# Joining the last stage of a two-layer graph kernel to its product stage, and starting that stage's gathers inside the layers

## The reference, cut to what matters

```python
def graph_conv(x, W, b):                      # three of these in a row, relu after the first two
    m = (x @ W)[src] * norm_src[:, None]
    return segment_sum(m, dst) * norm_dst[:, None] + b
x = layernorm(x + graph_conv3(x))             # (v - mean) / sqrt(var + 1e-5)

bf  = exp(coeff * (dist[:, None] - centers) ** 2)
bf  = ssp(bf @ V1 + c1); bf = ssp(bf @ V2 + c2)      # ssp(z) = softplus(z) - ln 2
msg = x[src] * edge_attr * bf * cutoff(dist)
agg = segment_prod(msg, dst)                  # product over a node's edges
x = layernorm(x + ssp(agg @ V3 + c3))
```

## Time and profile before

| | us |
|---|---|
| median of 3 runs | 4655.83 (4644.31 to 4661.99) |
| the profiled execution | 4661.2 |
| its span, first to last instruction | 4659.4 |

### The profile page before, as it was taken

How to read it: one execution, slowest core, us unless ns; L and a number is a source line. 1 busy time by engine, 2 the same in 40 slices (tenths; PEclk the granted TensorE clock), 3 DMA queues, 4 the chain that set the end, 5 groups by cost and what they waited for, 6 DMA issues and landing times. The chain is left out here.

```text
span 4659.4 us, 67064 instructions
## 1 busy us (share of the span) xinstructions
PE 3628.6 (78%) x23091; PEld 2344.5 (50%) x23091; DVE 3161.9 (68%) x5677; ACT 2724.9 (58%) x4265; POOL 1914.3 (41%) x1883
## 2 busy tenths in 40 slices
PE   5888889899999999999998566666666666666663
PEld 4777777444554455444544344444444444444442
DVE  9999999423333233332312788888888888888886
ACT  3666665322222222222200899999999989999983
POOL 6222000401000000100011677777777777777774
PEclk9888888999999999999999778788777778878775
DMA  4333333778887888887875666666666666666762
GB/s 139 131 134 131 124 129 129 239 242 250 247 248 225 245 246 245 249 247 243 248 229 167 193 198 194 199 195 202 197 195 200 199 195 199 195 198 194 201 186 76
DMA packets 641678, 920.75 MB, mean 198 GB/s; under 512 B 69714, under 2 KB 423239, under 8 KB 641431
## 3 DMA queue, kind: packets, MB, share of 16 engines
q1 hardware_dynamic: 550727, 782.85, 52.2%
q0 software_dynamic: 59936, 119.71, 10.9%
q10 hardware_dynamic: 30768, 15.26, 1.2%
HBM read 674.96 MB, written 242.59 MB: 197 GB/s over the span
## 5 line engine op out<-in xcount | busy, mean ns | idle before, releaser
L1311 POOL DMA_INDIRECT hgat<-x_rows,edge_src x1564 | 1504.6, 962 | 490.1 <-issue 475.1
L953 PE MATMUL bank<-gran,hp 128*128 128x490 bf16 x7056 | 1504.1, 372 | 28.6 <-DVE hp L1098 28.6
L953 PEld LDWEIGHTS bank<-gran,hp 128*128 128x128 bf16 x7056 | 677.3, 96 | 822.7 <-DVE hp L1098 30.1
L815 POOL DMA_INDIRECT x_sb<-h_rows,last_i x147 | 138.7, 943 | 1503.6 <-DMA h_rows<-h_out 1469.1
L1388 PE MATMUL bank<-c_b,one_b 96*128 96x512 bf16 x309 | 140.2, 454 | 744.4 <-DVE efl L1454 677.1
L1439 DVE TENSOR_SCALAR bank<-rows_e,edge_same,edge_first 128x128 f32<-128x128 f32 x1564 | 645.1, 412 | 42.5
L611 PEld LDWEIGHTS bank<-hi_hot,lo_hot 128*128 128x128 bf16 x7840 | 546.0, 155 | 217.8 <-issue 69.6
L611 PE MATMUL bank<-hi_hot,lo_hot 128*128 128x49 bf16 x7840 | 574.1, 219 | 94.7 <-DVE hi_hot L403 93.4
L527 ACT CAST stage<-bank 128x490 bf16<-128x490 f32 x784 | 451.9, 577 | 308.1 <-PE bank L611 297.4
L1019 DVE TENSOR_SCALAR t<-bank,c_sb 128x512 f32<-128x512 f32 x82 | 61.6, 751 | 826.3 <-PE bank L928 816.6
L1388 PEld LDWEIGHTS bank<-c_b,one_b 96*128 96x128 bf16 x309 | 30.5, 99 | 1019.9 <-issue 984.1
(11 more groups left out here) (237 smaller groups left out, 4485.9 us busy)
## 6 DMA issues: line engine op xcount, KB each, us to landing
gran<-step_counts SPq DMA_DIRECT2D x336, 857.5 KB, 4.9
dist<-weight_by_step SPq DMA_DIRECT2D x391, 256.0 KB, 4.6
running_products<-rows_e SPq DMA_DIRECT2D x391, 256.0 KB, 3.7
step_counts<-stage SPq DMA_DIRECT2D x112, 857.5 KB
ef<-in_edge_attr SPq DMA_DIRECT2D x391, 224.0 KB, 4.2
hgat<-x_rows,edge_src POOLq DMA_INDIRECT x1564
kn<-keep_and_norm_of_steps SPq DMA_DIRECT2D x48, 490.0 KB, 6.8
edge_filter_times_attr<-g_out SPq DMA_DIRECT2D x82, 256.0 KB, 3.5
```

The lines of the kernel that those rows point to most:

```text
L953: last = nc.tensor.matmul(y, hp[:, 7 * g + i, part, :], gran[:, g, :, i * IS:(i + 1) * IS], start=first, stop=last_)
L1311: pool.indirect_dma_start(out=hgat[:, b % U, c, :], out_offset=None, in_=x1_d, in_offset=bass.IndirectOffsetOnAxis(ap=edge_src[:, b, c:c + ...
```

## The change

- `hp1` loses its third part to a tile of its own, `third`, which outlives the layer stage; `hgat`, the ring of gathered rows, now lies in that tile's memory. Which part is meant is asked of `split_of`.
- At the end of the layer stage POOL waits until all of `x1_rows` is stored and then issues the 24 gathers of the ring's first six blocks (`gather_block`), still in the layer stage's `Block`. The product stage's POOL program starts at block 6.
- The late tiles 35 to 48 are cut at tile 45 (`LATE`, the first tile that needs the last block). `layer_norm` of tiles 35 to 41 and 42 to 44 moves into the last block, their root follows, and their ten tiles are normalised right after the last block's rows are biased; only four tiles stay behind the last gathers. There are eight stores of `x1_rows`.
- Roots: `exp(-0.5 * ln(var + eps))` on ACT, two instructions from the table that is loaded anyway; the add and the reciprocal on DVE and the square root go, in both stages. In the last stage there is one root per group.
- The last stage loses its own `Block` and stands behind the product stage's work in the same one; its loads of `v3` and `c3` come ahead of SP's last waits. `soft` now shares the memory of `prod`.
- In the last stage DVE normalises group g - 2 between `biased(g)` and `residual(g - 1)`.

```diff
+        U = 6
+        third = sb("third_of_hp1", [P, NT, D], BF16)
+        hgat = third[:].rearrange("p t d -> p (t d)").bitcast(F32)[:, 0:U * C4 * D].rearrange(
+            "p (u c d) -> p u c d", u=U, c=C4)
+        def gather_block(pool, b):
+            for c in range(C4):
+                pool.indirect_dma_start(out=hgat[:, b % U, c, :], out_offset=None, in_=x1_d,
+                                        in_offset=bass.IndirectOffsetOnAxis(ap=edge_src[:, b, c:c + 1], axis=0)
+                                        ).then_inc(s_gt[b % U], 16)
...
-            CUTS = (0, 35, NT)
+            LATE = next(t for t in range(NT) if blocks_for(t) == BLOCKS)
+            NORMS = [(7 * q, 7 * q + 7) for q in range(NG7 - 1)] + [(7 * NG7 - 7, LATE), (LATE, NT)]
+            ROOTS = ((0, 5), (5, 7), (7, 8))
...
+                    pool.wait_ge(s_x1d, 16 * len(NORMS))
+                    for b in range(U):
+                        gather_block(pool, b)
...
                     def root(i):
-                        act.wait_ge(s_rv, i + 1)
-                        nc.scalar.activation(rstd[:, CUTS[i]:CUTS[i + 1]], rstd[:, CUTS[i]:CUTS[i + 1]], ACT.Sqrt
-                                             ).then_inc(s_sd, 1)
+                        a, b = cuts(i)
+                        act.wait_ge(s_bn, 2 * ROOTS[i][1])
+                        nc.scalar.activation(rstd[:, a:b], mom[:, a:b, 1], ACT.Ln, bias=eps[:]).then_inc(s_lv, 1)
+                        act.wait_ge(s_lv, i + 1)
+                        nc.scalar.activation(rstd[:, a:b], rstd[:, a:b], ACT.Exp, scale=-0.5).then_inc(s_sd, 1)
...
+                            if n == 3 * BLOCKS - 1 and g == NG7 - 1:
+                                layer_norm(5)
+                                layer_norm(6)
                     post(At(3 * BLOCKS - 1))
                     bias_rows(2, At(3 * BLOCKS - 1))
-                    layer_norm(5)
-                    layer_norm(6)
-                    reciprocals(1)
                     normalise(1)
+                    layer_norm(7)
+                    normalise(2)
...
-                    for b in range(NB):
-                        if b >= U:
-                            pool.wait_ge(s_v, b - U + 1)
+                    for b in range(U, NB):
+                        pool.wait_ge(s_v, b - U + 1)
...
+                        gather_block(pool, b)
...
+                    for g, (a, b) in enumerate(groups):
+                        for t in range(a, b):
+                            pool.indirect_dma_start(out=prod[:, t, :], out_offset=None, in_=run_d,
...
+                    copy_turned(0)
+                    for g in range(NG):
+                        if g + 1 < NG:
+                            copy_turned(g + 1)
+                        softplus(g)
+                        if g:
+                            root(g - 1)
+                    root(NG - 1)
...
-        with ExitStack() as ph:
-            with nc.Block() as block:
...
                     for g in range(NG):
                         biased(g)
+                        if g >= 2:
+                            normalise(g - 2)
                         if g:
                             residual(g - 1)
-                        for i in range(2):
-                            if g == BATCHES[i][1]:
-                                reciprocals(i)
-                            if BATCHES[i][1] < g <= BATCHES[i][1] + 4:
-                                normalise(i, g - BATCHES[i][1] - 1 + BATCHES[i][0])
+                    normalise(NG - 2)
                     residual(NG - 1)
-                    reciprocals(2)
-                    for g in range(*BATCHES[2]):
-                        normalise(2, g)
+                    normalise(NG - 1)
```

More of the change, by code:

```diff
@@ L670, in gnn @@
             s_hst = [sem(f"s_h_stored{r}") for r in range(2)]
-            s_xg = [sem(f"s_x_gathered{q}") for q in range(NG7)]
+            s_xg = [sem(f"s_x_gathered{q}") for q in range(NG7 + 1)]
             s_hm, s_p1, s_h1, s_p2, s_hp = (sem(n) for n in (
@@ L694, in gnn, with split_of @@
             assert all(blocks_for(7 * q + 6) <= b - 1 for b, q in PARTS_AT.items())
+            def split_of(k, tiles, part):
+                if k % 2 == 0:
+                    return hp0[:, tiles, part, :]
+                return hp1[:, tiles, part, :] if part < 2 else third[:, tiles, :]
             class At:
@@ L911, in _ @@
                                     store_x1(q)
+                                root(1)
                     copy_h(2, At(BLOCKS * 3 - 1))
                     store_h(At(BLOCKS * 3 - 1), At(BLOCKS - 1))
-                    root(1)
-                    for q in range(5, NG7):
+                    for q in range(5, 7):
                         store_x1(q)
-                    act.wait_ge(s_x1d, 16 * NG7)
+                    root(2)
+                    store_x1(7)
+                    act.wait_ge(s_x1d, 16 * len(NORMS))
                     for r in range(2):
@@ L1096, in rest_h @@
                         dve.wait_ge(ready, NG7 * k + q + 1)
-                        into = part if nth == 0 else hps[k % 2][:, 7 * q:7 * q + 7, 2, :]
-                        nc.vector.tensor_tensor(into, part, hps[k % 2][:, 7 * q:7 * q + 7, nth, :], ALU.subtract
+                        into = part if nth == 0 else split_of(k, slice(7 * q, 7 * q + 7), 2)
+                        nc.vector.tensor_tensor(into, part, split_of(k, slice(7 * q, 7 * q + 7), nth), ALU.subtract
                                                 ).then_inc(signal, 1)
@@ L1241, in gnn @@
             s_fi = [sem(f"s_efl_in{r}") for r in range(U)]
-            s_gt = [sem(f"s_hgat{r}") for r in range(U)]
             s_rst = [sem(f"s_run_stored{r}") for r in range(U)]
@@ L1404, in _ @@
                     nc.tensor.transpose(banks[7][:, 0:P], ct[:, 0:P], ident[:]).then_inc(s_ctt, 1)
+                    pe.wait_ge(s_v3, 16)
+                    pe.wait_ge(s_x14, ND)
+                    pe.wait_ge(s_r1, ND)
+                    pe.wait_ge(s_r2, ND)
+                    pe.wait_ge(s_fin, ND)
+                    for g, (a, b) in enumerate(groups):
+                        pe.wait_ge(s_pg[g], 16 * (b - a))
+                        if g >= 2:
+                            pe.wait_ge(s_ptc, g - 1)
+                        for t in range(a, b):
+                            last = nc.tensor.transpose(banks[g % 2][:, (t - a) * P:(t - a + 1) * P], prod[:, t, :],
+                                                       ident[:])
+                        last.then_inc(s_pt, 1)
+                        pe.wait_ge(s_ptc, g + 1)
+                        if g >= ZB:
+                            pe.wait_ge(s_zs, g - ZB + 1)
+                        for t in range(a, b):
+                            last = nc.tensor.matmul(banks[2 + g % ZB][:, (t - a) * D:(t - a + 1) * D],
+                                                    prodT[:, g % 2, (t - a) * P:(t - a + 1) * P], v3_sb[:],
+                                                    start=True, stop=True)
+                        last.then_inc(s_z, 1)
                 @block.vector
```

217 lines of the change are left out of this document (79 added, 138 removed).

## The result

The changed kernel takes 4662.38 us in the median (4656.27 to 4668.47), the kernel before beside it 4655.51: ratio 1.0015, 95% interval 1.0008 to 1.0021. The forecast was 1.3 us faster; it became 6.9 us slower. The profiled execution of the changed kernel took 4663.31 us, with a span of 4661.5, against 4661.2 and 4659.4 before.

A forecast was written before the change was run, and what follows sets the result against it. The prediction took POOL's gather issue to pace the product stage and the last stage until its last gather. Its terms +3.6 - 3.2 - 1.7 = -1.3 us took the median 4655.8 to 4654.5 us, range 4642 to 4670.

The forecast's parts named there:

- part 2: Seam from layers to product stage: early gathers delay the barrier, POOL's 25th gather 3.6 us later, bounds 0.2 to 11.5.
- part 3: Seam to the last stage: next gather waits only for the scatter's landing, 3.2 us sooner, bounds 0 to 3.5.
- Part 1: End of the layer stage: only four tiles behind the last gathers, last store 4.1 us sooner.
- No second pause: Product stage: after its one hole POOL does not wait again; ACT and DVE catch up within 60 to 90 blocks.
- Part 4: Behind the last gather: fewer tiles left to normalise, 1.7 us less, bounds 0 to 3.5; removed table loads worth nothing.
- Rival (d): End of the kernel: output's way out bounds the tail, so nothing is gained there, 4656 us; chance 0.05.
- Rival (a): Product stage: the 29 us start lag of ACT and DVE stays, +24 us, 4680 us; chance 0.07.
- Rival (b): First seam: barrier is cheap and early gathers pay, some 5 us ahead, -9.6 us, 4646 us; chance 0.10.
- Rival (c): POOL's gathers change length as DVE's work beside them shifts phase, 28 us less, 4627 us; chance 0.06.

The follow-up runs named there:

- e12: Changed kernel with the loads of `v3` and `c3` moved to the start of the product stage; 4656.87 us, ratio 1.0003 to the kernel before.
- the control: The changed kernel run once more, unaltered, on the chip of other runs; 4666.41 us, ratio 1.0011 to the kernel before.
- e5: Changed kernel without early gathers and without POOL's wait for the `x1_rows` stores; 4652.43 us, ratio 0.9983 to the kernel before.
- e2: Changed kernel without early gathers, POOL's wait for the last `x1_rows` stores kept, on a slow chip; ratio 1.0002 to the kernel before.
- e10: Changed kernel without early gathers, POOL's wait for the last `x1_rows` stores kept, again on a slow chip; ratio 1.0000 to the kernel before.
- e13: Changed kernel without early gathers, POOL's store wait kept, on a chip where POOL sets the pace; ratio 0.9992 to the kernel before.
- e4: Changed kernel with POOL also waiting for its 24 early gathers to land before the barrier; 5045.61 us, one execution on a slow chip.

## Why the prediction was wrong

**The step that failed is the restart in part 2.** "I take 2.9 from the nearest row; ends: 0.4 (2598.0) and, if it counts from the last gather's landing, 4.2 (2601.8)": the barrier took 8.0 us, beyond both ends. From the last residual add, the 25th gather was forecast at +46.3 us and came at +52.4. The early gathers ended 1.3 us sooner than forecast (36.0 for 37.3 us behind the add), the barrier took 5.1 us more, and from the stage's start to the 25th gather it took 8.4 us for 6.1, since the first block's filter, issued behind four other loads, landed at 2609.1. The row I went by was the seam to the last stage, where POOL's DRAIN takes 2.5 us; in the layers' `Block` it already took 5.8 us behind the last gather in the kernel before, unseen because nobody waited, and 7.75 with 24 gathers more. The price of being last is not one number for every `Block`. The mechanism (the engines stand 30 us at the barrier, then POOL stands for them) was right, the term mis-sized: +9.7 for +3.6, in the measure from the layers' end. That is within its bounds (0.2 to 11.5), and enough by itself to turn the sum's sign.

**The second failure is a sentence of part 3**, "The loads of `v3` and `c3` were done long before." They are issued after the last block, 1.9 and 1.4 us ahead of the correction row's gather: +4.6 us in the trace, and in the time 4 to 6 by e12, not clear of noise. The sum had nothing for this wait. The wait that the change takes away (forecast -3.2, measured -3.3) was right, and this ate it.

**Part 1**: last store 3.6 us behind the last add by forecast, 3.8 measured. **No second pause**: right, no wait of POOL on products over 0.3 us after the 25th gather, and the end of the stage was POOL's. **Part 4**: -1.7 by forecast, -2.2 measured, with a single one-tile instruction at the end, as said. Rival (d) is out with that. The drain as long again that part 4 quotes for a table load isn't in the trace before: the load that starts at 4612.02 takes 1.28 us and the next copy on ACT starts at 4613.31. That changes nothing in the sum, as said there.

**Rival (a)** didn't come. **Rival (b)** would have needed the restart within a microsecond; it was the opposite. **Rival (c)** had the right mechanism and I gave it 0.06: what POOL lost in its long gathers is a matter of phase. The mean fell from 962 to 959 ns, some 5 us over 1564 gathers, which makes the -4.6 of the table, and in the last stage more of the gathers were held by DVE (9 long of 49 for 5), +2.7, though +0.4 in the control's profile. That these two are phase is argued from the line-up, not shown by a run of its own. "Nothing in the change alters how much DVE does beside those gathers" was true and no protection: it's when, not how much.

**Open.** What POOL's DRAIN does, why it takes 2.5 us at the end of the product stage's `Block` and 5.8 at the layers', and why it grows with the gathers before it (0.08 us each, by 5.8, 6.1 and 7.75). And what holds the engines on the two slow chips.

## What to carry to other kernels

Before work is put ahead of a barrier, look for which engine would be last at it, and read that engine's own DRAIN at this very `Block` in the trace, even where nobody waits for it yet: here it was POOL's, 5.8 us and more, with every engine's fill of the next stage behind it. Loads are not free in front of a small gather on which the path hangs; issue them a stage earlier. Where POOL's gathers pace a stage, line up the long ones with DVE's instructions and give the hot one a PSUM operand: that was worth 14 us, where the change was forecast to bring 1.3.

## What the runs showed of the hardware

- The barrier at a block's end: 3.0 us after the last store's issue with POOL there early (e5), 8.8 with POOL waiting for that store (e2, e10, e13), 8.0 after its last gather (6.3 with 4 gathers instead of 24).
- POOL's DRAIN at the end of the layers' `Block`: 5.8 us with no early gather, 6.1 with 4, 7.75 with 24, and 7.7 when all 24 had landed before it began (e4). At the end of the product stage's `Block`, in the kernel before, 2.5 us.
- A gather's landing went from 2.5 to 7.1 us behind a 256 KB broadcast load issued 1.4 us before it and a 64 KB load 0.5 us before that.
- A 128x512 f32 DVE product with both operands in SBUF holds a gather until its own end and 0.82 us; with one in PSUM it doesn't (mean 1.082 against 0.943 us). A cast and a normalising instruction with one large operand in SBUF held gathers too.
- The same program took 4655, 5041 and 5073 us on different chips.
